# Unread TensorE products ahead of some waits, and a later place for two VectorE scans

## What is computed

```python
# 1 tokens: a forward and a backward moving average, then a linear map 128 -> 256
fwd = ewma(x);  bwd = ewma(x reversed) reversed          # carry = 0.1 * x + 0.9 * carry
h = ((fwd + bwd) * 0.5) @ W.T + b
# 2 two layers of a selective scan over time, on layernorm(h)
for l in range(2):
    delta = softplus(hidden @ Wd + bd);  u = hidden @ Wi + bi
    state = scan(exp(-delta * softplus(A_log)), delta * u)      # s = d * s + g
    hidden = state @ Wo + bo + (last state @ Ws + bs)
h = h + hidden
# 3 on layernorm(h): a shared expert of width 512, and 4 of 16 routed experts of width 64
h = h + (silu(z @ G.T) * (z @ U.T)) @ Down.T + sum over the 4 of weight * expert(z)
```

## Time and profile before

| | us |
|---|---|
| runs before | 1292.98 median of 3 (1288.44 to 1296.14) |
| profiled execution, its own time | 1287.21 |
| its span, first to last instruction | 1285.2 |
| TensorE busy | 1167.1, 91% of the span |
| VectorE busy | 925.4, 72% |
| mean granted TensorE clock | 0.950 of full speed |

### The profile page before, as it was taken

One profiled execution on the slowest core, in us unless ns is written; L12 is line 12 of the kernel. 1 busy time (PEld: TensorE's weight loads), 2 busy tenths in 40 slices (PEclk: granted clock), 3 DMA queues, 4 the chain that ended last, 5 costly groups with the idle time before them and its releaser, 6 DMA issues.

```text
span 1285.2 us, 24806 instructions
## 1 busy us (share of the span) xinstructions
PE 1167.1 (91%) x7501; PEld 1050.6 (82%) x7501; DVE 925.4 (72%) x2361; ACT 557.7 (43%) x913; POOL 403.4 (31%) x282
## 2 busy tenths in 40 slices
PE   5379867988999989998999899998999999999997
PEld 4248746867998789988988799978998899899997
DVE  8665998689758984889678985798578755644443
ACT  2623642562355433653365244553366343223332
POOL 2022172033211723144412523153302431262323
PEclk9658886997999999999999999999999999999999
DMA  4121021122022423231221322231221321243331
GB/s 127 42 64 41 17 71 37 44 71 74 9 49 40 106 51 54 42 76 55 36 70 32 80 54 54 42 98 37 53 50 41 83 38 38 54 110 57 54 53 18
DMA packets 88288, 71.48 MB, mean 56 GB/s; under 512 B 39671, under 2 KB 82848, under 8 KB 88168
## 3 DMA queue, kind: packets, MB, share of 16 engines
q1 hardware_dynamic: 58832, 43.30, 12.2%
q0 software_dynamic: 26832, 26.06, 12.1%
q10 hardware_dynamic: 2504, 0.55, 0.2%
HBM read 31.36 MB, written 39.34 MB: 55 GB/s over the span
## 4 chain that ended last, share of the span: by engine, by line
PE 67%; DVE 23%; issue 6%; ACT 2%; POOL 1%; DMA 0%; ACTq 0%; DVEq 0%; POOLq 0%
PE gu_ps L1745 18%; PE gu_ps L1718 15%; PE d_ps L1821 10%; PE d_ps L1802 8%; PE ch_ps L1695 3%; PE ch_ps L1789 3%; PE ch_ps L1621 2%; PE ch_ps L1681 1%; DVE h L1243 1%; PE ch_ps L1781 1%; DVE h L1511 1%; DVE gu_ps L1500 1%; DVE stats L1249 1%; PE ch_ps L1651 1%; PE ch_ps L1639 1%
## 5 line engine op out<-in xcount | busy, mean ns | idle before, releaser
L832 POOL DMA_INDIRECT out_dram<-block_rows,entry x99 | 158.2, 1598 | 323.6 <-ACT block_rows L992 303.2
L1745 PE MATMUL gu_ps<-gu_hi,bx_hi 128*128 x792 | 235.3, 297 | 1.9 <-issue 1.8
L980 ACT ACTIVATE hid<-gu_ps 128x512 f32<-128x512 f32 (+1 forms) x195 | 115.2, 593 | 271.4 <-PE gu_ps L1745 174.4
L1745 PE MATMUL gu_ps<-gu_lo,bx_hi 128*128 x792 | 225.3, 284 | 0.0
L1745 PE MATMUL gu_ps<-gu_hi,bx_lo 128*128 x792 | 224.9, 284 | 0.0
L813 POOL DMA_INDIRECT lists<-records,pos x96 | 126.7, 1320 | 191.4 <-DVE pos L1408 165.8
L1802 PE MATMUL d_ps<-down,hid 128*125 128x256 f32 x768 | 184.4, 384 | 0.0
L1745 PEld LDWEIGHTS gu_ps<-gu_hi,bx_hi 128*128 128x128 f32 x792 | 151.9, 192 | 7.0 <-issue 5.9
L1802 PEld LDWEIGHTS d_ps<-down,hid 128*125 128x125 f32 x768 | 140.7, 191 | 19.1 <-issue 0.3
L1745 PEld LDWEIGHTS gu_ps<-gu_hi,bx_lo 128*128 128x128 f32 x792 | 151.9, 192 | 0.9
L1745 PEld LDWEIGHTS gu_ps<-gu_lo,bx_hi 128*128 128x128 f32 x792 | 150.9, 191 | 0.0
(11 more groups left out here) (282 smaller groups left out, 2859.0 us busy)
## 6 DMA issues: line engine op xcount, KB each, us to landing
block_rows<-lists SPq DMA_DIRECT2D x99, 128.0 KB, 3.7
out_dram<-h SPq DMA_DIRECT2D x24, 500.0 KB
t<-rstd_scratch SPq DMA_DIRECT2D x21, 250.0 KB, 5.2
x_in<-in_x_dram SPq DMA_DIRECT2D x8, 375.0 KB, 7.6
zt<-in_x_dram SPq DMA_DIRECT2D x7, 375.0 KB, 3.6
entry<-lists SPq DMA_DIRECT2D x99, 8.0 KB, 3.0
out_dram<-block_rows,entry POOLq DMA_INDIRECT x99, 3.8
lists<-records,pos POOLq DMA_INDIRECT x96, 4.2
```

Source lines behind the costliest of these rows:

```text
L832: pool.indirect_dma_start(out=out_rows[0:there, :], out_offset=bass.IndirectOffsetOnAxis(entry[n % UE][:, ID:ID + 1].bitcast(U32), 0), in_ ...
L980: inc(act.activation(hid[g % 4][:, 0:n], gu_ps[:, 2 * (g % 2), 0:n], ACT.Silu), "silu_done")
L1745: last = pe.matmul(gu_ps[:, 2 * (g % 2) + half, q * GH:(q + 1) * GH], a[n % 2][:, k, :], w[:, k, bass.ds(of, 1), half * GH:(half + 1) * GH ...
```

## The change

Two parts. (1) `WARM`, `WARM_TOKW` and `WARM_UP` name places in TensorE's order at which it issues extra products whose results nobody reads: `tw_hi` by `tw_hi` (f32r, 128 by 128 by 256 columns), or ident by ident (f32, 128 columns) where the weights do not exist yet. They go into the bank that the next real product overwrites, behind the wait that frees this bank and ahead of the wait for the next step's data; those in `BESIDE` go into a bank of `gu_ps` and stand ahead of the wait for the bank. There are 335 of the first kind (`WARM` without `tok` 0 of pair 0: 75, 58, 13, 22, 8, 36, 44, 5; `WARM_UP`: 20, 42, 12) and 19 of the second. `WARM_UP` (pair, n) adds besides a wait for `silu_done` of the slot before, because the bank is that slot's. (2) `ewma` 1 and `ewma_back` 1 of VectorE move from tick -28.5 to -28.0 and -27.5; new entries in `EARLY` keep pairs 0 to 2 where they were, so that pairs 3 to 7 change. `ewma` 1 then stands behind `block_lo` of one tick and ahead of `block_hidden` part 1 of the next, `ewma_back` 1 behind `tok` 0 and `tok` 1.

```diff
--- before.py
+++ after.py
@@ -21,11 +21,11 @@
 CHAIN = (
     ("ewma", 0, dict(SP=-32.5, DVE=-33.5, POOL=-29.0, ACT=-29.5)),
     ("ewma_back", 0, dict(DVE=-32.0)),
-    ("ewma", 1, dict(SP=-27.0, DVE=-28.5, POOL=-27.0, ACT=-27.0)),
+    ("ewma", 1, dict(SP=-27.0, DVE=-28.0, POOL=-27.0, ACT=-27.0)),
     ("tok", 0, dict(PE=-28.0, DVE=-27.5)),
     ("tok", 1, dict(PE=-27.5, DVE=-27.5)),
     ("tok", 2, dict(PE=-26.5, DVE=-26.5)),
-    ("ewma_back", 1, dict(DVE=-28.5)),
+    ("ewma_back", 1, dict(DVE=-27.5)),
     ("tok", 3, dict(PE=-25.0, DVE=-25.0)),
     ("pre", (0, 0), dict(PE=-19.5, DVE=-19.5)),
     ("ln1_part", 0, dict(DVE=-25.0, POOL=-25.0)),
@@ -176,7 +176,10 @@
     (1, "spread", 0): dict(SP=-26.0),
     (0, "split", (1, 0)): dict(ACT=-6.5, DVE=-8.0),
     (0, "carry", 0): dict(DVE=-14.0, PE=-13.5),
-    (0, "ewma", 1): dict(SP=-24.0),
+    (0, "ewma", 1): dict(SP=-24.0, DVE=-28.5),
+    (1, "ewma", 1): dict(DVE=-28.5),
+    (1, "ewma_back", 1): dict(DVE=-28.5),
+    (2, "ewma_back", 1): dict(DVE=-28.5),
     (0, "pre", (1, 0)): dict(DVE=-13.0),
     (0, "pre", (1, 1)): dict(DVE=-12.5),
     (0, "ssm_decay", 1): dict(DVE=-10.0),
@@ -205,7 +208,7 @@
     (0, "ln1_part", 1): dict(POOL=-20.5),
     (2, "list", 7): dict(POOL=15.5),
     (0, "tok", 1): dict(DVE=-27.0),
-    (2, "ewma", 1): dict(ACT=-28.0),
+    (2, "ewma", 1): dict(ACT=-28.0, DVE=-28.5),
     (2, "split", (0, 0)): dict(ACT=-14.0),
     (0, "pre", (0, 1)): dict(PE=-19.5),
     (1, "ln1_part", 1): dict(DVE=-24.0),
@@ -245,6 +248,24 @@
 )
 
 CLASSES = ((0, 1), (0, 2), (0, 3), (1, 2), (1, 3), (2, 3))
+
+
+
+WARM = {
+    (0, "tok", 0): 8,
+    (0, "carry", 0): 75,
+    (0, "class_row", 0): 58,
+    (0, "y", (0, 0)): 13,
+    (0, "y", (2, 0)): 22,
+    (1, "tok", 2): 8,
+    (1, "y", (0, 0)): 36,
+    (2, "tok", 1): 44,
+    (2, "tok", 2): 5,
+}
+BESIDE = ((0, "y", (2, 0)), (1, "tok", 2), (2, "tok", 1), (2, "tok", 2))
+
+WARM_TOKW = (6, 5, 0)
+WARM_UP = {(0, 6): 20, (0, 11): 42, (1, 11): 12}
 
 
 def audio_tower_kernel(nc, x, tok_w, tok_b, wd, bd, wi, bi, a_log, wo, bo, ws, bs, router_w, corr_bias,
@@ -1553,9 +1574,30 @@
             pe.wait_ge(S["ident_done"], 2)
             pe.wait_ge(S["pool_const"], 2)
 
+            def warm(bank, many):
+                for _ in range(many):
+                    pe.matmul(bank[:, 0:D], tw_hi[:, 0:P], tw_hi[:], start=True, stop=True)
+
+            def warm_ident(bank, many):
+                for _ in range(many):
+                    pe.matmul(bank[:, 0:P], ident[:], ident[:], start=True, stop=True)
+
+            def warm_beside(pair, many):
+                if pair < 2:
+
+                    wait(pe, "shared_hi", 4)
+                    wait(pe, "shared_lo", 4)
+                    warm(gu_ps[:, 3, :], many)
+                else:
+
+                    g = slot_of["S", pair - 2, NT * M - 2]
+                    wait(pe, "silu_done", done(g))
+                    warm(gu_ps[:, 2 * (g % 2), :], many)
+
             def prepare(what, n):
                 if what == "tokw":
                     bank = fold_ps[n]
+                    warm_ident(bank, WARM_TOKW[n])
                     if n == 0:
                         pe.wait_ge(S["w_tok"], 16)
                         for k in range(KD):
@@ -1610,8 +1652,15 @@
                     inc(last, "shared_mm")
 
             def chain(step, arg, pair):
+                many = WARM.get((pair, step, arg), 0)
+                if (pair, step, arg) in BESIDE:
+                    warm_beside(pair, many)
                 bank_is_free(pe, step, arg, pair)
                 bank = ch(step, arg, pair)
+                if (pair, step, arg) == (0, "tok", 0):
+                    warm_ident(bank, many)
+                elif (pair, step, arg) not in BESIDE:
+                    warm(bank, many)
                 if step == "tok":
                     if arg % 3 == 0:
                         wait(pe, "ew_lo_done", 2 * pair + arg // 3 + 1)
@@ -1724,6 +1773,10 @@
                 banks_of_slot(g)
                 inc(product(gu_ps[:, 2 * (g % 2), 0:TT], gate_hi, gate_lo), "half_mm")
                 between(amid, g)
+                if (pair, n) in WARM_UP:
+
+                    wait(pe, "silu_done", done(g - 1))
+                    warm(gu_ps[:, 2 * ((g + 1) % 2), :], WARM_UP[pair, n])
                 wait(pe, "hid_done", done(g - 2))
                 groups(g + 1)
                 inc(product(gu_ps[:, 2 * (g % 2) + 1, 0:TT], up_hi, up_lo), "prod_mm")
```

## The result

The changed kernel takes 1287.01 us (median of 20 runs, 1284.28 to 1291.97), the kernel before 1292.99 in the same series (20 runs, 1287.79 to 1299.58). The ratio is 0.9957, with a 95% interval of 0.9945 to 0.997. That is a gain of 6.0 us; the forecast was 13, so 1280 was 7 us too low, and 0.43% lies within the 0.5% that the prediction called no difference (the interval, all the same, leaves out a ratio of 1).

A forecast was written before the change was run, and what follows sets the result against it. TensorE at 1.2 GHz after waits was taken to bound slow early stretches. Terms 10.0 + 0.7 - 0.8 + 1.7 + 1.5 = 13.1 us took 1287.2 to 1274.1; with the median 5.8 above, 1280 us, range 1268 to 1291.

The forecast's parts named there:

- Rival (a): Unread products themselves run at 1.2 GHz and outlast their waits: 20.7 us together, no gain, 1314 us; chance 0.07.
- Setup and `carry`: Pair 0's start: `carry`, transposes and `pre` run at 2.4 GHz, gaining 2.0 us, between 0 and 3.4.
- rival (b): VectorE and ScalarE also pace pair 0; only setup's, pair 2's and the scans' gains stay: 1289 us; chance 0.11.
- `y`, 4.6 us: Pair 0: six counted halves of `y` at 2.4 GHz save 4.9 us, less 0.3 for the first's wait.
- `y` (2, 0) and `logit`, 1.6 and 1.6: Pair 0: two more `y` halves save 1.6 us; `logit` at twice the clock saves 1.6 at best.
- The rest of the prelude, 1.6: Pair 0 after `logit`: 12 `tok` products and another `y`, 2.7 us by TensorE, taken as 1.6 because of VectorE.
- Slot 6, 0.7: Pair 0, n = 6: 20 products in a wait of 3.16 us gain 0.7 us, between 0 and 2.9.
- Slot 11, -0.8: Pair 0, n = 11: 42 products start late and delay pair 1's `y`: 0.8 us lost, between 1 gained and 6 lost.
- Pair 2's prelude: 44 and 5 products in waits let TensorE run at 2.4 GHz up to 220 us: 1.7 us gained, between 0 and 4.5.
- The scans, 1.5 us: Pairs 3 to 7: moved scans exchange waits, gaining 0.3 us five times; between 4.5 gained and 6.5 lost.
- Rival (c): Moved scans cost 1.3 us at each of five places as the clock falls; 11.6 us gain elsewhere stays: 1288; chance 0.10.
- rival (d): The median's 5.8 us above the profile are slow clock stretches the products remove too: 1274 us; chance 0.15.

The follow-up runs named there:

- one_row_carry: The changed kernel with 22 plain f32 one-row products ahead of `carry` in place of the 75 f32r ones: 1294.46 us, ratio 1.0.
- row125_only: The kernel before, with only pair 0's class row added to `y` by a product over 125 rows instead of one: 1287.44 us, ratio 0.9937.
- row_as_125: The changed kernel with pair 0's class row added to `y` by a product over 125 rows instead of one: 1280.05 us, ratio 0.9902.
- fewer: Changed kernel, class row by 125 rows, slot 11's products in a free bank, pair 1's `tok` 1 filled, 117 other unread products removed: 1274.65 us, ratio 0.9863.
- scans_only: The kernel before with only the two scans of pairs 3 to 7 moved, no unread products: 1289.39 us, ratio 0.9978.
- products_only: The changed kernel with the scans back in their old place: 1288.60 us, ratio 0.9968.
- row125_slot11: The changed kernel with the class row by 125 rows and slot 11's 42 products in the free bank, without `silu_done` wait: 1277.98 us, ratio 0.9873.
- best_old_scans: The changed kernel with class row by 125 rows, slot 11's products in the free bank, scans in their old place: 1278.33 us, ratio 0.9886.
- slot11_early: The changed kernel with slot 11's 42 products in the free bank of `class_row`, without the wait for `silu_done`: 1283.55 us, ratio 0.9926.

## Why the prediction was wrong

**The unread products run at 2.4 GHz and fit their waits** (right for the 75, 58, 44, 22 and 20). `carry`'s 75 took 9.2 us from 36.0 to 45.2 (forecast 9), and its wait went from 11.7 to 1.9 us. Besides the 42 of slot 11, the 13 ahead of `y` (0, 0) ran at 1.2 GHz: 3.14 us against the 2.20 that TensorE waited there before, and the first `y` came 0.4 us later than before (67.39 against 66.95). So did the 12 of slot (1, 11), which stood behind `silu_done` too. The 36 ahead of `y` of pair 1 ran at 2.4 GHz, but some 2.5 us beyond their wait. Rival (a), 0.21 us each everywhere, fell. (Its 4.5 us at `carry` should be 4.1: 75 at 0.21 are 15.8, less 11.7.)

**Setup and `carry`, 2.0 us** (the size was off: 0.2). The clock fell at 48.1, right behind the 1.9 us of wait that was left, and the state scan came only 0.2 us sooner: VectorE and ScalarE pace this stretch, as rival (b) had it for all of pair 0.

**`y`, 4.6 us** (the step that failed: 2.2). The prediction saw that the one-row products "seem to do less" for the clock in the earlier trace rows, took it for a doubt, and priced it at 1.4 us off 11.4. It was the main effect. The clock rose at 68.6 us and fell at 72.0: three halves ran at full speed, not eight. one_row_carry shows that these products do not hold the clock, row125_only that removing them does what the unread products were there for. The fall at 69.0 in row_as_125 shows that they are not the only thing that brings the clock down in this run; what differs is whether it comes back inside it. The row of 70 to 80 us had it all: 10.0 of 10 us busy at 0.50 can't be cured by keeping TensorE busier ahead of it.

**`y` (2, 0) and `logit`, 1.6 and 1.6** (right: 1.6 and 1.3). **The rest of the prelude, 1.6** (wrong sign: -0.6), and **the first slot, costed at nothing** (1.7 us lost). The clock had fallen again at 95.9 behind `y` (2, 0), and rose at 106.1. The first slot had run at full speed before; the prediction counted only where work would be sped up, and not that work which comes sooner can come ahead of the clock's rise. At the first gate product 4.6 us were there, behind the first slot 2.9, where 10.0 had been put, below the lower end of 4.

**Slot 6, 0.7** (0.3, in its bounds). **Slot 11, -0.8** (right mechanism, wrong size: -3.1, within the -6). The unread products began late and at the lower clock, as worked out (42 in 7.8 us, between the 6 and 9 given). What was off is what contention would give back: the table and the split did become short (0.18 and 0.93 us, as said), but VectorE had stood 5.88 us idle before them, and for 1.56 more behind the 36 products; the sum counted on nearly all of that delay being absorbed. The rule on VectorE and GpSimd (the Trainium skill, SBUF — State Buffer, section Who interferes with whom) thus held for the two steps, and was no price for the idle time ahead of them. The sign put down for it, a wait of 0.6 us ahead of the 42 products, was wrong too: the whole wait, 5.86, stands there.

**Pair 2's prelude, 1.7** (1.9 in the profile; but without its products, in fewer, the same stretch still gains 0.7 us and the median loses nothing, so that this gain isn't shown to be the products').

**The scans, 1.5 us** (1.4 to 2.8 by three pairs of medians, of which one is clear of no gain; the waits changed places as described). The traces do not say where it comes from: from pair 1's first gate product to the end, which holds all five places, moving the scans lost 0.7 us in scans_only, gained 3.0 in the changed kernel against products_only, and gave 0.0 in row125_slot11 against best_old_scans. So the size fits and the mechanism, 0.3 us in each of five places, isn't shown. Rival (c) was right that the clock falls at the new waits: in the changed kernel it fell at all five (310.9, 454.3, 597.6, 737.6 and 880.9 us). But in the kernel before it fell at three of the four old ones as well (595.6, 735.6, 878.9), and the time did not get longer.

**The readings of the rows.** "From the eleventh slice on it stands at full speed" reads too much into the digit 9, which is 90% or more: from 321 to 1280 us the clock of the kernel before was 0.99 in the mean, with some 14 us at 1.2 GHz in four places. And 1268 is the sum of the best ends of the terms (24.3 us) with the median's 5.8 us left as they are; with rival (d) it would be 1263.

**The sum.** 13.1 was forecast, 3.9 is in the span: 7.1 of the missing 9.2 us are pair 0, 2.3 slot 11. **The median** was put 5.8 us above the profile and stood 2.1 above, so 3.7 us of gain came in that the sum had left out. Rival (d) spoke of this; but the profiled runs of row_as_125, slot11_early and fewer stand 2.8, 2.2 and 2.1 us *above* their medians, so one profiled run's place among the others tells nothing, and why this distance shrank is open. That 1287 lies inside the range, and close to the 1289 and 1288 of rivals (b) and (c), is luck: neither describes what the trace shows, and without these 3.7 us the gain would have been 2.3.

The rule of the Trainium skill that the prediction cites for the clock's ramp (TensorE: Matmul & The Clock Gate, section What's actually happening) gave an estimate of 12.9 us at most. The fastest version gains 17, about 15 without the scans, a part of it from products that are shorter at either clock. So no run here shows that estimate broken; but it was no reason to take 13 for reachable by this change.

## What to carry to other kernels

Before filling waits to hold the clock, look at what TensorE does in the slow stretch: where it is busy without a gap and still at 1.2 GHz, change the form of those products; here the one-row form cost time at either clock and the clock as well. Put fillers only where their bank is free without waiting for another engine, and sum up who waits behind them. And follow a gained microsecond up to the next full-speed stretch: work that arrives before the clock has risen gives it back.

## What the hardware did that was not expected

- TensorE busy without a gap, with plain f32 products of one row, went to 1.2 GHz and stayed there: for 15 us in one_row_carry, where it fell 2.2 us after they began, and from 72.0 us on in the changed kernel, where they stand between f32r ones. The clock rose inside the `y` run with 125 rows, at 70.6 in row125_only and at 72.4 in row_as_125.
- A one-row product is not cheaper. Half a `y` takes 1.05 us with one-row products and 0.67 with 125 rows at 2.4 GHz, 1.86 and 1.28 at 1.2.
- Filling a wait all but 2 us did not keep the clock: it fell 1.0 us behind a wait of 1.9 at `carry` and in one of 2.3 at `class_row`. Behind the 42 products of slot11_early a wait of 1.5 us was left, and the clock stayed at 1.00.
- 354 unread products gave 4 us of 1293 by ratio (products_only); two lines that changed the form of twelve products in pair 0 gave 8 (row125_only).
